# Moving edge work, target ids, the edge count and TensorE's tail order in a four-block graph kernel

## The reference, cut to what matters

```python
# block 0: masked attention (8 heads of 64), then a feed-forward part
q, k, v = x @ Wq + bq, x @ Wk + bk, x @ Wv + bv
adj[src, dst] = 1
attn = softmax(where(adj[:, None, :] == 0, -1e9, q.k / 8), axis=heads)
h1 = layer_norm(x + (attn @ v) @ Wo + bo) * g1 + be1
x = layernorm(x + (layer_norm(h1 + relu(h1 @ W1 + b1) @ W2 + b2) * g2 + be2))
# block 1: 4096 edges, edge_attr has 64 columns; W1 has 2*512 + 64 rows
h = mish(concat(x[src], x[dst], edge_attr) @ W1 + b1)
m = mish(h @ W2 + b2)
agg = segment_sum(m, dst)
x = layernorm(x + (layer_norm(x + mish(concat(x, agg) @ W3 + b3) @ W4 + b4) * gamma + beta))
# block 2: two graph convolutions (Ahat: the normalised adjacency with loops)
x = layernorm(x + (Ahat @ relu(Ahat @ (x @ G1) + b1) @ G2 + b2))
# block 3: own and neighbours' mean (Cn: counts over the degree)
x = layernorm(x + (layernorm(x @ Ws.T + (Cn @ x) @ Wn.T + bias) * gamma + beta))
```

## Time and profile before

| what | us |
|---|---|
| median of 3 runs | 239.29 (237.8 to 240.47) |
| the profiled execution | 241.44 |
| its span, first to last instruction | 239.6 |
| PE busy in it | 228.1 (95%) |
| DVE busy | 169.3 (71%) |
| ACT busy | 128.7 (54%) |
| mean granted PE clock, share of full | 0.988 |

### The profile page before, as it was taken

How to read it: one execution, slowest core, us unless ns; L and a number is a source line. 1 busy time by engine, 2 the same in 40 slices (tenths; PEclk the granted TensorE clock), 3 DMA queues, 4 the chain that set the end, 5 groups by cost and what they waited for, 6 DMA issues and landing times.

```text
span 239.6 us, 3302 instructions
## 1 busy us (share of the span) xinstructions
PE 228.1 (95%) x1237; PEld 184.8 (77%) x1237; DVE 169.3 (71%) x304; ACT 128.7 (54%) x238; POOL 5.5 (2%) x17
## 2 busy tenths in 40 slices
PE   8999999996999999999999999999999999999980
PEld 4866779763766887888888888888888888998770
DVE  2958786778579655886876967868568646556695
ACT  0626489548449835745635646547475533148700
POOL 1000010001000000000000000000000000000001
PEclk9999999999799999999999999999999999999997
DMA  7999999497300940019031050088000000000001
GB/s 229 279 395 398 392 386 406 145 316 277 133 0 0 358 170 0 0 21 330 2 102 74 3 175 1 0 286 282 3 0 0 0 3 0 0 4 0 0 3 44
DMA packets 12759, 31.26 MB, mean 130 GB/s; under 512 B 1068, under 2 KB 1988, under 8 KB 11720
## 3 DMA queue, kind: packets, MB, share of 16 engines
q1 hardware_dynamic: 11952, 30.54, 35.8%
q10 hardware_dynamic: 792, 0.51, 0.8%
HBM read 30.79 MB, written 0.26 MB: 130 GB/s over the span
## 4 chain that ended last, share of the span: by engine, by line
PE 81%; DMA 6%; DVE 5%; SPq 2%; issue 2%; ACT 1%; POOL 1%; POOLq 0%; DVEq 0%; ACTq 0%
PE bank L733 36%; PE bank L716 13%; PE bank L539 6%; DMA Wv<-in_L_gnn_Wv 4%; PE bank L530 4%; PE bank L571 3%; PE bank L743 3%; PE bank L744 3%; DMA ids<-in_dst 2%; PE bank L612 2%; PE bank L754 1%; PE bank L519 1%; PE bank L693 1%; PE bank L694 1%; SPq L248 1%
## 5 line engine op out<-in xcount | busy, mean ns | idle before, releaser
L733 PE MATMUL bank<-W2hi,Hhi 128*128 128x512 f32 x128 | 49.8, 389 | 0.0
L733 PE MATMUL bank<-W2hi,Clo 128*128 128x512 f32 x128 | 49.8, 389 | 0.0
L733 PE MATMUL bank<-W2lo,Hhi 128*128 128x512 f32 x128 | 49.8, 389 | 0.0
L427 ACT ACTIVATE Mhi<-M 128x512 fp32r<-128x512 f32 x32 | 20.2, 632 | 44.3 <-DVE M L1122 44.3
L1127 DVE TENSOR_TENSOR Mlo<-M,Mhi 128x512 fp32r<-128x512 f32 x32 | 22.1, 690 | 16.3 <-ACT M L428 16.3
L1122 DVE TENSOR_TENSOR M<-bank,b2r 128x512 f32<-128x512 f32 x32 | 22.0, 688 | 12.6 <-PE bank L744 7.6
L733 PEld LDWEIGHTS bank<-W2hi,Clo 128*128 128x128 f32 x128 | 24.0, 188 | 5.0
L733 PEld LDWEIGHTS bank<-W2hi,Hhi 128*128 128x128 f32 x128 | 24.0, 188 | 5.0
L733 PEld LDWEIGHTS bank<-W2lo,Hhi 128*128 128x128 f32 x128 | 24.0, 188 | 5.0
L334 ACT ACTIVATE C<-bank,cols 128x512 f32<-128x512 f32 x32 | 19.7, 694 | 15.1 <-PE bank L571 15.1
L420 ACT ACTIVATE Hhi<-C 128x512 fp32r<-128x512 f32 x32 | 20.0, 624 | 11.4 <-DVE C L1108 11.1
(11 more groups left out here) (242 smaller groups left out, 340.2 us busy)
## 6 DMA issues: line engine op xcount, KB each, us to landing
F<-in_L_gnn_W SPq DMA_DIRECT2D x2, 2048.0 KB, 17.3
W1raw<-in_L_gnn_W SPq DMA_DIRECT2D x1, 2048.0 KB, 21.9
ids<-in_src SPq DMA_DIRECT2D x2, 1024.0 KB, 13.4
ids<-in_dst SPq DMA_DIRECT2D x2, 1024.0 KB, 6.3
dst_ids<-in_dst SPq DMA_DIRECT2D x2, 1024.0 KB, 7.4
src_ids<-in_src SPq DMA_DIRECT2D x1, 2048.0 KB, 8.2
W<-in_L_gnn_W SPq DMA_DIRECT2D x1, 2048.0 KB, 8.8
Wq<-in_L_gnn_Wq SPq DMA_DIRECT2D x4, 256.0 KB, 5.2
```

The lines of the kernel that those rows point to most:

```text
L427: act.activation(Mhi[:, t, :], M[:, t, :], ACT.Mish)
L733: done = mm(ST2[t][:, :], x[:, c, e], w[:, c, :], start=c == 0 and i == 0, stop=c == KC - 1 and i == 2)
```

## The change

1. **Edge count.** On PE, `count_edges` moves from behind `v` to ahead of it; on ACT the copies `CTs` and `uniform` move ahead of the exponentials.
2. **Target ids.** The first half of the target ids has a place of its own (`first_dst`) and is loaded behind `F2`. DVE compares it between the third and the fourth pair of `W1lo`. The second half goes to `ids0`; `W2raw` is issued before it. `W2hi` on ACT waits for all eight pieces of one-hots, where it waited for six.
3. **Edge steps and features.** Step 5 leaves the second half of `F2` and joins steps 6 to 10 behind it. `turn_features(3)` with its copies moves from ahead of `F2` to behind step 10, into bank 2, and `ea` moves to another place in SBUF. B waits for it (`ea_lo`).
4. **DVE.** `w2_low((0, 1))` moves behind the four copies of B.
5. **Tail.** On PE, the turns 6 and 7 move: 6 behind the bias row, 7 behind g3. Both halves of the bias row come ahead of g1, half 0 of `xw` ahead of g2. Bank 2 takes the place of bank 6. `keep_warm` has 4 instead of 5.

No operation is added or taken away but one `keep_warm` multiply; 1 MB of target ids is loaded at another time.

```diff
@@ sync
             sp.wait_ge(S["ct_done"], 1)
             sp.dma_start(F2, w_view(a["L0_gnn_W2"])).then_inc(S["f2_in"], 16)
+            sp.dma_start(early_ids["first_dst"], by_partition(a["dst"][0:E // 2], E // 2)).then_inc(S["dst_ids_in0"], 16)
             sp.wait_ge(S["wo_done"], 2)
...
-            for h in range(2):
-                sp.wait_ge(S["st_ready"], 2 * (h + 1))
-                sp.dma_start(other[f"ids{h}"], by_partition(a["dst"][E // 2 * h:E // 2 * (h + 1)], E // 2)).then_inc(S[f"dst_ids_in{h}"], 16)
+            sp.wait_ge(S["st_ready"], 2)
             sp.dma_start(W2raw, w_view(a["L1_gnn_W2"])).then_inc(S["w2_in"], 16)
+
+            sp.wait_ge(S["st_ready"], 4)
+            sp.dma_start(other["ids0"], by_partition(a["dst"][E // 2:], E // 2)).then_inc(S["dst_ids_in1"], 16)
@@ scalar
+            act.wait_ge(S["ct_done"], 1)
+            act.activation(CTs[:, :], bank[0][:, 0:N], ACT.Copy).then_inc(S["ct_read"], 1)
+            act.wait_ge(S["eighth"], 1)
+            act.activation(uniform[:, :], bank[0][:, 0:N], ACT.Relu, bias=eighth[:, 0:1], scale=-1.0 / HEADS).then_inc(S["uniform_ready"], 1)
             for o in range(2):
                 act.wait_ge(S["s_centred"], o + 1)
...
+            edge_term_out(range(4, RING_STEPS - 1))
             features_high(3)
-            edge_term_out(range(4, RING_STEPS))
+            edge_term_out(range(RING_STEPS - 1, RING_STEPS))
             act.wait_ge(S["w2_in"], 16)
-            act.wait_ge(S["st_ready"], 6)
+            act.wait_ge(S["st_ready"], 8)
@@ tensor
             done.then_inc(S["scores_done"], 1)
+            pe.wait_ge(S["onehot_bf"], 2)
+            count_edges(range(ET)).then_inc(S["ct_done"], 1)
...
             pe.wait_ge(S["ff_ready"], FC - 2)
-            turn_features(3)
             pe.wait_ge(S["f2_in"], 16)
             for h in range(2):
                 columns_by((bank[1], bank[2]), ffT, F2, h, range(0, 3), 0, FC - 1)
-                edge_term(range(h + 4, h + 5))
+                if h == 0:
+                    edge_term(range(4, 5))
...
-            edge_term(range(6, 8))
+            edge_term(range(5, 8))
             pe.wait_ge(S["graph_ready"], 2)
-            pe.wait_ge(S["ea_lo"], PAIRS)
             edge_term(range(8, RING_STEPS - 1))
+
+            pe.wait_ge(S["stat_ready"], 2)
+            turn_features(3)
             pe.wait_ge(S["pre_read"], 18)
...
-            for q in range(TURNED_FIRST + 1, 2 * KC):
-                turn(q)
+
+            g_banks = (bank[5], bank[2])
...
+            start_with(g_banks, row["L2_gnn_b2"])
+            turn(2 * KC - 2)
             pe.wait_ge(S["r0_ready"], 1)
             mm(bank[3][:, 0:HID2], Ahat[:, :], r0, start=False, stop=True).then_inc(S["g1_done"], 1)
...
             for h in range(2):
-                mm((bank[5], bank[6])[h][:, 0:D // 2], p1g, half(G2, h), start=False, stop=True).then_inc(S["g3_done"], 1)
-
+                mm(g_banks[h][:, 0:D // 2], p1g, half(G2, h), start=False, stop=True).then_inc(S["g3_done"], 1)
+
+            turn(2 * KC - 1)
             pe.wait_ge(S["wt_ready"], 2 * KC)
             pe.wait_ge(*row_in["L3_gnn_bias"])
             start_with((bank[4], bank[0]), row["L3_gnn_bias"])
-            keep_warm(5, bank[1])
+            keep_warm(4, bank[1])
@@ vector
             for c in range(2 * KC):
+                if c == 2 * KC - 2:
+                    first_onehots(DT_by_tile, dst_halves, "dst_ids_in", 0)
                 dve.wait_ge(S["w1_hi"], c // 2 + 1)
...
-            st = residual((bank[1], bank[2]), xw, S["f2_done"], lambda: first_onehots(DT_by_tile, "dst_ids_in", 0))
+            st = residual((bank[1], bank[2]), xw, S["f2_done"])
...
             out_halves(xT_flat, xs_banks, S["nT_done"], 2, S["nT_ready"])
-            first_onehots(DT_by_tile, "dst_ids_in", 1)
+            features_low(3)
+            first_onehots(DT_by_tile, dst_halves, "dst_ids_in", 1)
```

More of the change, by code:

```diff
@@ L96, in gnn_kernel @@
                        ("Hhi", 56, 8, F32R), ("M", 64, 4, F32), ("Mhi", 68, 4, F32R), ("b2r", 72, 1, F32), ("AB", 87, 4, F32R))
-        first = overlay(("Wq", 0, 4, F32), ("Wk", 4, 4, F32), ("Wv", 8, 4, F32), ("ea", 12, 4, F32), ("F1", 16, 8, F32),
+        first = overlay(("Wq", 0, 4, F32), ("Wk", 4, 4, F32), ("Wv", 8, 4, F32), ("ea", 44, 4, F32), ("F1", 16, 8, F32),
                         ("F2", 24, 8, F32), ("MA", 48, 4, F32), ("W2raw", 52, 4, F32), ("attn", 56, 2, F32), ("Wo", 60, 4, F32),
@@ L113, in gnn_kernel @@
         thin = overlay(("bvo", 87, 2, F32), ("bvo_parts", 89, 2, F32R))
+        early_ids = overlay(("first_dst", 52, 4, I32))
         loop_ids = overlay(("src_ids", 73, 8, I32), ("dst_ids0", 81, 4, I32), ("dst_ids1", 91, 4, I32))
@@ L142, in gnn_kernel @@
         dst_ids = [loop_ids[f"dst_ids{h}"].rearrange("p (e q i o) -> p q o i e", q=PAIRS, i=GT, o=2) for h in range(2)]
+        dst_halves = [x.rearrange("p (e q i o) -> p q i o e", q=PAIRS, o=2, i=GT) for x in (early_ids["first_dst"], other["ids0"])]
         row_ids = [other[f"ids{h}"].rearrange("p (e q i o) -> p q i o e", q=PAIRS, o=2, i=GT) for h in range(2)]
@@ L164, in gnn_kernel @@
         AGG, ST1, ST2 = bank[0], bank[5:8], (bank[3], bank[4], bank[1], bank[2])
-        EA_BANKS = (bank[4], bank[4], bank[3], bank[3])
+        EA_BANKS = (bank[4], bank[4], bank[3], bank[2])
         F1_BANKS = bank[1:5]
@@ L382, in _ @@
             act.activation(v_sb, bank[3][:, :], ACT.Copy).then_inc(S["v_ready"], 1)
[L383 to L386, removed]
             act.wait_ge(S["wo_in"], 16)
@@ L689, in _ @@
             for b, c0 in ((bank[1], 0), (bank[2], KC)):
+                if c0:
+                    pe.wait_ge(S["ea_lo"], PAIRS)
                 for c in range(KC):
@@ L845, in _ @@
             pe.wait_ge(*row_in["L2_gnn_b2"])
-            mm(bank[5][:, 0:D // 2], ident[:, :], half(row["L2_gnn_b2"], 0), start=True, stop=False)
+            start_with(g_banks, row["L2_gnn_b2"])
+            turn(2 * KC - 2)
             pe.wait_ge(S["r0_ready"], 1)
             mm(bank[3][:, 0:HID2], Ahat[:, :], r0, start=False, stop=True).then_inc(S["g1_done"], 1)
-            pe.wait_ge(S["wt_ready"], KC + 3)
-            mm(bank[6][:, 0:D // 2], ident[:, :], half(row["L2_gnn_b2"], 1), start=True, stop=False)
+            pe.wait_ge(S["xw_ready"], 2)
+            mm(g_banks[0][:, 0:D // 2], ident[:, :], half(xw, 0), start=False, stop=False)
             pe.wait_ge(S["g1_ready"], 1)
             mm(bank[4][:, 0:N], r1g, Ahat[:, :], start=True, stop=True).then_inc(S["g2_done"], 1)
-            for h in range(2):
-                pe.wait_ge(S["xw_ready"], 2 + h)
-                mm((bank[5], bank[6])[h][:, 0:D // 2], ident[:, :], half(xw, h), start=False, stop=False)
+            pe.wait_ge(S["xw_ready"], 3)
+            mm(g_banks[1][:, 0:D // 2], ident[:, :], half(xw, 1), start=False, stop=False)
             pe.wait_ge(S["g2_ready"], 1)
             for h in range(2):
-                mm((bank[5], bank[6])[h][:, 0:D // 2], p1g, half(G2, h), start=False, stop=True).then_inc(S["g3_done"], 1)
+                mm(g_banks[h][:, 0:D // 2], p1g, half(G2, h), start=False, stop=True).then_inc(S["g3_done"], 1)
+            turn(2 * KC - 1)
             pe.wait_ge(S["wt_ready"], 2 * KC)
@@ L920, in bank_statistics, with residual @@
                 return stats.rearrange("p h s -> p (h s)")
-            def residual(banks, extra, signal, between=None):
+            def residual(banks, extra, signal):
                 for h in range(2):
-                    if h == 1 and between:
-                        between()
                     dve.wait_ge(signal, h + 1)
@@ L1052, in _, with first_onehots @@
             v.tensor_scalar(Ahat[:, :], mask[:, :], small[:, 2:3], None, ALU.mult).then_inc(S["graphT_ready"], 1)
+            def first_onehots(by_tile, halves_of, arrived, h):
+                dve.wait_ge(S[f"{arrived}{h}"], 16)
+                for q in range(2):
+                    v.tensor_scalar(by_tile[:, q, h], halves_of[h][:, q], iota_col[:, 0:1], None, ALU.is_equal).then_inc(S["st_ready"], 1)
             for c in range(2 * KC):
+                if c == 2 * KC - 2:
+                    first_onehots(DT_by_tile, dst_halves, "dst_ids_in", 0)
                 dve.wait_ge(S["w1_hi"], c // 2 + 1)
                 v.tensor_tensor(W1lo[:, c, :], W1raw[:, c, :], W1hi[:, c, :].bitcast(F32), ALU.subtract).then_inc(S["w1_lo"], 1)
[L1057 to L1063, removed]
             for h in range(2):
-                first_onehots(ST_by_tile, "row_ids_in", h)
+                first_onehots(ST_by_tile, row_ids, "row_ids_in", h)
             dve.wait_ge(S["graphT_done"], 1)
@@ L1096, in _ @@
             v.tensor_tensor(Alo, bank[1][:, :], Ahi.bitcast(F32), ALU.subtract).then_inc(S["ab_ready"], 1)
-            w2_low((0, 1))
             dve.wait_ge(S["ab_done"], 2)
@@ L1102, in _ @@
```

(5 more changed lines are left out.)

6 lines of the change are left out of this document (2 added, 4 removed).

## The result

| kernel | median, us | executions |
|---|---|---|
| before | 240.00 (237.8 to 241.76) | 20 |
| changed | 238.33 (237.6 to 238.92) | 20 |

The ratio of changed to before is 0.9947, with a 95% interval of 0.9925 to 0.9969: about 1.3 us faster, where the forecast was 2.5. The plain medians lie 1.7 us apart, because that of before falls into a gap: 8 of its 20 executions took 239.35 us or less, 10 took 240.26 or more. The time of 238.33 lies inside the predicted range. The profiled execution took 237.9 us, with a span of 236.1 (before 241.44 and 239.6).

What follows compares the result with a forecast made beforehand. PE, busy for 95% of the span, was taken to bound the kernel. 241.44 - 1.7 - 1.6 + 0.8 = 238.9 us profiled; the same 2.5 us from 239.29 gives 236.8, range 235.4 to 239.6.

Steps and rivals of the forecast that it cites:

- the sum: Whole kernel: 241.44 - 1.7 - 1.6 + 0.8 = 238.9 us profiled; the same 2.5 us from 239.29 gives 236.8.
- Block 0, -0.5: Block 0: count fills PE's wait for Wv, v's products start earlier; 0.5 us gained, 0.2 if v's copy is late.
- Ids and LN2, -1.7 for the start of A: LN2: earlier xs and six edge steps in the wait start product A 1.7 us earlier, block 0's 0.5 included.
- The clock, -1.6: Product A behind LN2: without the 1.84 us stand-still PE keeps full clock, 1.6 us gained.
- Rival B: LN2: the clock gives nothing, as before's median doesn't lose it or the new gaps do; 238.4 us, chance 22%.
- The tail, +0.8: Tail: turn 7 behind g3 delays ACT's queue and xThi, block 3 starts later; 0.8 us lost, bounds 0.4 and 1.1.
- Rival C: Tail: costs little (0.2 us), since ACT's block slides under the warm-up; 236.2 us, chance 12%.
- Rival D: LN2: rows land late, LN2 loses 1.9 us, clock falls again; 240.3 us, 241.8 with tail clock loss; chance 6%.
- Rival E: Tail: the low clock comes there alone, 1.5 us lost; 238.3 us, chance 10%.

Runs made afterwards that it cites:

- the ids alone: The kernel before with part 2 alone (first half of target ids in its own place, no compare between the residual's halves): 237.75 us, ratio 0.9898.
- the count first: The kernel before with part 1 alone (edges counted ahead of v, copies of the counts ahead of the exponentials): 240.47 us, ratio 1.0028.
- the new tail: The kernel before with part 5 alone (the change's tail, old order at LN2): 239.71 us, ratio 1.004.

## Why the prediction was right and wrong

**The step that failed** is the one from the profiled execution to the median: "The profiled execution is 2.15 us above the median of the runs shown; the same 2.5 us from 239.29 gives 236.8." It takes the 2.15 us as an offset that stays. In truth they were in large part the very losses that the change removes: above all the low clock in A, which the sum took off every execution. Against the lower group of before the sum is right: 240.7 - 238.3 = 2.4 us, forecast 2.5. But 25 of 52 executions weren't in that group, and against them the change gives 238.6 - 238.3 = 0.3. By the group means before has a mean of (27 x 240.7 + 25 x 238.6) / 52 = 239.7, and 238.3 / 239.7 = 0.994, close to the measured 0.9947.

**Block 0, -0.5.** Right for the execution shown (8.28 - 7.76 = 0.52), mis-sized for others: 0.17. Of the difference of 0.35 us, 0.28 is the wait for `Wv`, which the three other profiles of the old order don't have. The lower bound of 0.2 fits, but it was given for another reason, a late copy of v.

**Ids and LN2, -1.7 for the start of A.** Right for the execution shown: A started 45.04 us behind the scores, now 43.10, a gain of 1.9. Against the old order at full clock (57.47 - 13.05 = 44.42) it is 1.3: 0.35 of the gain was that execution's block 0, 0.27 its longer stand-still. The path was as described, but what PE waited for last at the turning of `xs` was ACT. All PE rows lie 0.87 us earlier for the scores' sake; with that added, the second source half is waited for until 46.99 (forecast 46.7), the residual begins at 50.05 (49.8), PE turns `xs` at 55.92 (55.7), and A starts at 57.41 (57.6). Of the parts of this term the ids carried 0.8 (50.98 - 50.16), and the sixth step nothing. The rows had said so: ACT needs 1.17 us a step against PE's 0.89, and a sixth step in the wait is one more that ACT holds up.

**The clock, -1.6.** The mechanism held: clock 1.00 in A, and 0 of 20 executions in the lower group. Only its share in the median was wrong, 27 of 52 instead of all. Rival B, which had 22%, names this condition; its 238.4 is what came. That its number fits so well is in part luck: it starts at 239.29 where the upper group has 238.6, and takes off 1.7 where 1.3 is the gain at full clock. The three times shown (237.8, 239.29, 240.47) already spanned both groups, and of the two readings of that spread the text took the one that the single profile showed. The Trainium skill (TensorE: Matmul & The Clock Gate, Part 1) says that the chip's watching isn't tied to the kernel's start. By that the same order can come out both ways, and 27 of 52 agrees.

**The tail, +0.8.** Right, by the path described: 0.94 measured. Turn 7's copy was forecast 5.9 us behind z and came at 5.97; ACT had no gap up to `xThi`; PE waited 0.69 us for the bank (forecast 0.9) and at block 3 for ACT's `xThi`. The forecast of 0.76 was short by 0.2, inside its bounds of 0.4 and 1.1. Rival C, a tail that costs little, is out.

**Rival D**, rows that land late, is out for the changed kernel: DVE had no wait for the row. With the ids alone it waited 0.31 us, so the margin was thin. **Rival E**, the low clock in the tail, is out: no execution of 20 was in the lower group, and PE had clock 1.00 behind its wait of 0.69 us in the profile. So the 1.5 us that D and E put on it stays an estimate.

## What to carry to other kernels

Before a loss in one profiled execution is booked, ask whether the shown times can all contain it. Here three times spread over 2.7 us, a lost clock costs 2.1, and it was in only half of the executions; the sum should have started from each group by itself, weighted. An engine's idle time can be filled for free only as far as the engine that drains its results keeps up. And a step that is moved later on one engine pulls the whole queue of its reader with it: count what stands behind the copy in that queue, down to the first thing that the path needs.

## What the runs showed of the hardware

- One order, two outcomes: after a stand-still of 1.84 and of 1.76 us PE worked at the lower level (granted clock 0.50, multiplies 0.42 us apart instead of 0.23), after one of 1.57 it kept clock 1.00. The lower group held 27 of 52 executions of before, 9 of 11 with the count first, 3 of 11 with the new tail. Since the tail comes later than LN2, 3 of 11 against 27 of 52 is perhaps chance. Whether the moment or the length of the stand-still decides in one execution stays open: the two profiles with the longer ones have the low clock, and the unprofiled executions don't show theirs. With the ids alone, whose profile has 0.70 us, the lower group held none of 12.
- Issuing a DMA can hold SP for long. SP's issue rows of the changed kernel (start, us):

```profile
16.63 3.50 SPq L262 DMA_DIRECT2D F<-in_L_gnn_W  x1
20.17 9.65 SPq L263 DMA_DIRECT2D first_dst<-in_dst  x1
29.86 1.23 SPq L266 DMA_DIRECT2D ids<-in_src  x2
```

and in the kernel before:

```profile
21.90 0.37 SPq L259 DMA_DIRECT2D F<-in_L_gnn_W  x1
```

The issue of `first_dst`, 1 MB behind `W1raw` and `F2`, took 9.65 us (7.54 with the ids alone), while in the kernel before `F2`, issued later, took 0.37. The source ids behind it slid a little: they were issued at 29.86, against 29.21 before and 28.40 with the count first, and DVE waited 1.29 us for their second half. PE's rows show no loss from it, since its turning of `xs` at 55.05 was released by ACT.
